# Unread matmuls in the typed attention stage of a graph and expert network on one core

## The reference

```python
q_att = jnp.einsum('nhd,rhde->rnhe', q, relation_att)
attn_score = jnp.sum(q_att[etype, col_idx] * k[row_idx], axis=-1)
score = attn_score * (relation_pri[etype] / SQRT_DK)
m = jax.ops.segment_max(score, col_idx, num_segments=n)
ex = jnp.exp(score - m[col_idx])
denom = jax.ops.segment_sum(ex, col_idx, num_segments=n)
agg = jax.ops.segment_sum((ex / denom[col_idx])[..., None] * msg_edge, col_idx, num_segments=n)
```

## Time and profile before

| | us |
|---|---|
| median of 3 runs | 5765.59 |
| lowest and highest | 5760.42, 5766.13 |
| span of the profiled execution | 6191.8 |
| typed scores in it (first spread to last maximum) | 2394 to 3152 |
| typed weights in it | 3174 to 3271 |
| typed sums in it | 3275 to 3505 |

### The profile page before, as it was taken

One profiled execution on the slowest core, in us unless ns is written; L12 is line 12 of the kernel. 1 busy time (PEld: TensorE's weight loads), 2 busy tenths in 40 slices (PEclk: granted clock), 3 DMA queues, 4 the chain that ended last, 5 costly groups with the idle time before them and its releaser, 6 DMA issues. The chain is left out here.

```text
span 6191.8 us, 76002 instructions
## 1 busy us (share of the span) xinstructions
PE 4533.9 (73%) x22806; PEld 3190.3 (52%) x22842; DVE 3374.5 (55%) x7236; ACT 1645.9 (27%) x3766; POOL 2414.1 (39%) x2719
## 2 busy tenths in 40 slices
PE   5877978757758694566558889998999495354468
PEld 1223434545546452444436677777888363344456
DVE  8988972645556654677757743342111333544454
ACT  0964652411213251011100133333222121100022
POOL 0851018545540534555500028861122301577710
PEclk8988989868878897666758989999999697677779
DMA  0002447422232388777746410004333332233310
GB/s 31 2 11 102 190 181 210 157 45 39 41 60 79 100 322 277 236 246 240 242 132 218 149 25 12 17 7 129 100 110 120 91 100 61 91 91 90 92 29 21
DMA packets 413215, 696.03 MB, mean 112 GB/s; under 512 B 116843, under 2 KB 301299, under 8 KB 408203
## 3 DMA queue, kind: packets, MB, share of 16 engines
q1 hardware_dynamic: 316322, 440.23, 22.7%
q0 software_dynamic: 96320, 250.79, 13.5%
q10 hardware_dynamic: 192, 0.15, 0.0%
HBM read 450.69 MB, written 239.64 MB: 111 GB/s over the span
## 5 line engine op out<-in xcount | busy, mean ns | idle before, releaser
L1109 PE MATMUL wsum_a_ps<-wsum_a_hot,wsum_a_rows 128*128 128x128 f32 x1664 | 290.4, 349 | 359.7 <-DVE big L1136 185.7
L2242 POOL DMA_INDIRECT big<-hgt_table,edge_key x416 | 394.2, 948 | 364.4 <-DVE hgt_s_tmp L2335 221.0
L1095 POOL DMA_INDIRECT wsum_a_rows<-table,edge_src x416 | 434.2, 1044 | 221.9 <-issue 165.5
L1109 PEld LDWEIGHTS wsum_a_ps<-wsum_a_hot,wsum_a_rows 128*128 128x128 f32 x1664 | 272.1, 257 | 378.0 <-issue 210.0
L3928 PE MATMUL sagel_ps<-sagel_piece,sagel_high 128*128 128x448 f32 x1050 | 399.0, 380 | 0.8 <-issue 0.8
L3928 PE MATMUL sagel_ps<-sagel_piece,sagel_low 128*128 128x448 f32 x1050 | 385.2, 367 | 0.0
L2325 DVE TENSOR_REDUCE hgt_highest<-hgt_s_pm 128x8 f32<-128x1024 f32 x208 | 253.3, 1219 | 188.3 <-remote 181.6
L2242 POOL DMA_INDIRECT big<-gat_table,own_src x288 | 272.5, 946 | 211.6 <-issue 82.0
L2292 PE MATMUL hgt_s_pq<-big 128*128 x1248 | 249.9, 372 | 136.0 <-DVE hgt_s_tmp L2335 75.6
L2282 PE MATMUL hgt_s_pm<-hgt_s_turned,pick 112*128 112x128 bf16 x1664 | 188.5, 282 | 216.9 <-DVE hgt_highest L2325 185.3
L790 PE MATMUL cnt_ps<-cnt_hot_s,cnt_hot_d 128*128 128x512 bf16 (+1 forms) x1724 | 309.8, 333 | 39.0 <-DVE cnt_hot_s L772 34.9
(11 more groups left out here) (1007 smaller groups left out, 10909.7 us busy)
## 6 DMA issues: line engine op xcount, KB each, us to landing
hgt_edge_values<-big SPq DMA_DIRECT2D x104, 512.0 KB
big<-hgt_edge_values SPq DMA_DIRECT2D x104, 512.0 KB, 4.6
x<-counts SPq DMA_DIRECT2D x75, 448.0 KB, 3.3
x<-counts SPq DMA_DIRECT2D x75, 336.0 KB, 2.9
counts<-big SPq DMA_DIRECT2D x25, 832.0 KB, 3.4
counts<-big SPq DMA_DIRECT2D x25, 768.0 KB, 3.3
big<-counts SPq DMA_DIRECT2D x30, 640.0 KB
counts_turned<-big SPq DMA_DIRECT2D x30, 640.0 KB
```

The lines of the kernel that those rows point to most:

```text
L1095: nc.gpsimd.indirect_dma_start(rows[n % DEEP][:, u, :], None, table, bass.IndirectOffsetOnAxis(ap=e.src[:, g:g + 1], axis=0)).then_inc(gat ...
L1109: mm = nc.tensor.matmul(ps[r.slot % 2][u][:, k * P:(k + 1) * P], rows[r.slot][:, u, k * P:(k + 1) * P], hot[r.slot % 2][:, u, :], start=Tr ...
L2242: nc.gpsimd.indirect_dma_start(rows[n % DEEP][:, u, :], None, at.table, bass.IndirectOffsetOnAxis(ap=at.index[:, g:g + 1], axis=0)).then_i ...
```

## The change

An eighth PSUM bank, `idle`, is taken in both typed functions. In TensorE's step of `hgt_s` one matmul into it comes behind `lay_out(0)` and three behind `lay_out(1)`; in `hgt_w` four come behind each batch's last matmul. Each has the bf16 identity (112 x 128) as weights and 512 columns of `kit.pick` as moving operand. Both are constants, so these matmuls wait for nothing and raise no semaphore, and nothing reads the bank. The builder calls TensorE's step 109 times for the 104 rounds (it fills and drains the pipeline), which makes 436 matmuls in the scores, and 104 in the weights.

Beside that, five waits against a register's value now have the value masked by a bitwise AND that leaves it as it is.

```diff
+def not_below_zero(value, highest):
+    return value & ((1 << highest.bit_length()) - 1)
...
 # build_counts, VectorE, each visit
-                            dve.wait_ge(moved, buckets[u] + 1)
+                            dve.wait_ge(moved, not_below_zero(buckets[u], 2 * NT - 1) + 1)
 # build_counts, ScalarE, each of 50 parts
-                    wait_alone(act, done, end + BASE)
+                    wait_alone(act, done, not_below_zero(end, visits) + BASE)
...
 # edge_scores
+        idle = c.enter_context(nc.psum_tensor(f"{nm}_idle", [P, 512], F32)) if at.dots else None
...
+                    def turn_over(times):
+                        if idle is not None:
+                            for n in range(times):
+                                nc.tensor.matmul(idle[:], kit.ident16[0:PICK_ROWS, :],
+                                                 kit.pick[:, 4 * n:4 * n + 4, :].rearrange("p n q -> p (n q)"),
+                                                 start=True, stop=True)
...
                     lay_out(0)
+                    turn_over(1)
                     if before.there:
...
                     lay_out(1)
+                    turn_over(3)
...
 # edge_weights, behind the 16 matmuls of a batch
                     mm.then_inc(spread, 1)
+                    for n in range(4):
+                        nc.tensor.matmul(idle[:], kit.ident16[0:PICK_ROWS, :],
+                                         kit.pick[:, 4 * n:4 * n + 4, :].rearrange("p n q -> p (n q)"),
+                                         start=True, stop=True)
...
 # edge_sums, TensorE, each matmul; ScalarE, each of 25 blocks
-                            pe.wait_ge(moved, blocks[u] + 1)
+                            pe.wait_ge(moved, not_below_zero(blocks[u], NT - 1) + 1)
-                    wait_alone(act, done, end + BASE)
+                    wait_alone(act, done, not_below_zero(end, groups) + BASE)
```

More of the change, by code:

```diff
@@ L2576, in edge_weights @@
         pd_v = [p[:, 0:B * 3 * H].rearrange("p (g k h) -> p g k h", k=3, h=H) for p in pd]
+        idle = c.enter_context(nc.psum_tensor(f"{nm}_idle", [P, 512], F32))
         made, spread, summed, shifted, under, raised = sems(nc, c, nm, "made spread summed shifted under raised")
```

## The result

| | before | after |
|---|---|---|
| median, us | 5764.27 (16 runs, 5755.89 to 5776.72) | 5777.16 (16 runs, 5771.26 to 5782.24) |
| ratio to before, 95% interval | | 1.0021 [1.0014, 1.0027] |
| span of the profiled execution, us | 6191.8 | 5775.9 |

The change costs 12.9 us, 0.21%. The prediction was 5787 us, 21 us more than before, in the range of 5725 to 5840. The sign is right, but the next sections show that the sum is made of the wrong parts.

The account below looks back on a forecast made before the run. VectorE's round of 5.07 us was taken to bound the typed scores, TensorE's sequencer the typed weights. Terms 9 + 8 + 4 + 0 = 21 us on 5765.6 gave 5787 us, range 5725 to 5840.

Parts of the forecast that it names:

- Typed scores, +9 us: Four added matmuls a round: VectorE's 5.07 us round covers them at full clock; six half-clock rounds cost 1.56 us each.
- the sum of 4.5 us for TensorE's round: Typed scores at full clock: 2.33 us spread and first lay_out, about 0.9 turn and second, 1.22 for four added matmuls.
- Gain from the clock, 0: Typed scores: a faster TensorE gains nothing, since rounds at half and full clock both take 5.07 us.
- The first rival: Half clock does hold the typed scores' rounds up, so full clock makes the kernel faster, about 5744 us; chance 0.25.
- Typed weights, +8 us: Four added matmuls a batch: TensorE's sequencer sets the pace and issues each in 0.076 us, over 26 batches.
- Masks in the sums, +4 us: Typed sums: only the first of a round's four masks counts, 0.07 us each, half of it over 104 rounds.
- Masks in the counts, 0: Counts: VectorE's 629 ns instructions cover the added register operation; 31 us if that cover were gone.
- The late completions: VectorE's waits ending by "remote", in typed scores, weighted sums and untyped scores, 503 us, largely of the profiled execution alone.
- the second rival: The late completions are real and come with clock changes; a steady clock ends them, about 5560 us; chance 0.05.
- The third rival: Typed scores: the clock falls all the same, half the rounds stay at half clock, 81 us, 5859 us; chance 0.08.

Follow-up runs that it names:

- sixteen: The changed kernel with sixteen unread matmuls a round in the typed scores in place of four, none in the typed weights: 5861.97 us, ratio 1.0168 to before.
- masks only: The changed kernel without any unread matmul in scores or weights, its masks kept: 5778.48 us, ratio 1.0019 to the kernel before.

## Why the prediction came out as it did

**Typed scores, +9 us: wrong, it is 0.** The mechanism was right (VectorE's round covers TensorE up to a point, and beyond it the product waits for `hgt_s_pq`, as sixteen show), and the clock did stay at 1.00 while VectorE was full. Two sizes were off. A matmul costs 0.216 us at full clock, not 0.31, and the sum of 4.5 us for TensorE's round counted the tail of every group: TensorE is busy 302.0 of 400 us, 3.8 us of a round of 5.07. The cover is thicker than 0.6 us: four more matmuls still fit. And six rounds at half clock were charged, where the 400 us have none. The 0.98 of the whole stage is some 20 us at half clock at its two ends (0.67 in 2245 to 2255 and in 2780 to 2790), where VectorE is not full (3.76 and 7.58 of 10 us) and the one wait for `hgt_s_pq` there, 0.9 us, is in masks only too.

**Gain from the clock, 0: right.** The rows of both kernels at 0.83 and 1.00 show it over 400 us, where the prediction had two rounds. The Trainium skill, "TensorE: Matmul & The Clock Gate", section "Why this matters for your kernels", advises to keep TensorE free of idle gaps between bursts. The unread matmuls do that, the clock in the trace is 1.00 in place of 0.83, and there is no gain, since VectorE sets the round. The first rival (5744 us) is refuted: it decides where VectorE waits for `hgt_s_pq`, and it waits 0.9 us for it in the whole stage.

**Typed weights, +8 us: wrong, it is 0.** The step said the sequencer sets the pace and then charged four more items to it. But the stage did not grow (97.2 against 97.1): the unread matmuls run on the array while the sequencer is at the next batch's register operations.

**Masks in the sums, +4 us: mechanism wrong, size near.** Measured 6 (235.3 against 228.9, masks only 234.8). "Only the first of a round's four masks stands behind the wait for new data" is the step that failed: the first and the last cost the same. The price of 0.07 us was low as well (0.092 to 0.097), and taking half of it had no ground in the rows. The four cost little because the stream had 0.40 us a round to spare, and 4 x 0.097 us nearly used that up; that 4 came out near 6 is luck.

**Masks in the counts, 0: wrong, 3 to 4 us.** 352.0 and 353.0 against 348.7, and 7.5 more for a second mask. "The operations in front have always been ready early" was read from 0.4 us of "issue" on L772 alone. That row does not see the place where it counts, the change from the short L765 to the first L772 of four and from the last L772 back to L765. 440 operations of 0.07 to 0.09 us on VectorE would be 31 to 40 us if none were covered, so most are.

**The late completions.** The prediction took them to be of the profiled execution alone. Twelve further profiled executions, of the changed kernel and eleven variants, have none in the typed scores, and spans of 5771 to 5863 us that go with their timed medians; one of them, masks only, has no unread matmuls and a clock of 0.83, and takes 552.0 us for the stage. So neither the matmuls nor a steady clock ended them, which refutes the second rival (5560 us). As far as thirteen profiles can say, they were a matter of that one execution; what caused them is open. Before itself was not profiled a second time, so that its scores take 550 us in timed runs is argued, not seen: from masks only, from the 426 us, and from the granted clock of the whole program, which is 0.872 in before's timed runs and 0.871 in those of masks only, but 0.845 in before's profiled execution. The prediction's line that these waits "should still be there" contradicts its own reading, and failed.

**The third rival** (clock falls, 5859 us) is refuted by the window: 1.00.

The whole: masks 6 + 3 to 4 = about 10 us by stages, 11 by the timed ratio of masks only (0.0019 x 5765), of 12.9 us; the remaining 2 us are inside the intervals. The prediction had put 17 of its 21 us on the unread matmuls, which cost nothing, and 4 on the masks, which cost all. That the sum has the right sign and lies 8 us off is luck.

## What to carry to other kernels

Filling an engine's gaps to lift its clock is worth only what someone waits for on that engine: read whether the consumer is busy without gaps before counting on it. Register operations in a hot loop are work on the engine's own instruction stream, here 0.07 to 0.10 us each, and in the sums they were nearly free only while that stream still waited for data at the loop's head; count them all, before and after the wait. Where the engine's instructions are short, as at the change between the two groups in the counts, they can cost although longer instructions around them cover theirs. And when a profiled span is hundreds of microseconds away from the timed runs, compare stages only with the executions whose span fits.

## What the runs showed of the hardware that was not expected

An execution with completions up to six microseconds late stood 426 us above the timed runs of the same kernel, and none of the twelve other profiled ones looked like it. Sixteen unread matmuls in a batch of 3.86 us cost 0.17 us of it: the clock rose from 0.50 to 1.00 with them, and one took 0.23 us in place of 0.47; four left it at 0.50. A second AND before each of a round's four matmuls cost 36.5 us over 104 rounds where the first had cost 6. One more semaphore wait that was already met cost as much as one AND, 0.08 us a round.
